# Where a hybrid attention layer finishes its mixed rows: in the merging of triangular blocks, or in the recurrence

## The reference, cut to what matters

```python
q, k, v = (silu(causal_conv4(x @ W.T)) for W in (Wq, Wk, Wv)); beta = sigmoid(x @ Wb.T)
# delta rule by chunks (q, k normalised, v and kb = k scaled by beta):
T = inverse_of_unit_triangular(kb @ k.T);  u = T @ v;  w = T @ kb
for each chunk:
    u_i = u - w @ S;  o = q @ S + masked(q @ k.T) @ u_i;  S = S + k.T @ u_i
paths  = (fir3(v), fir63(v), delta, v)
logits = gelu([x, mean and variance of each path and head] @ gate_w1.T + b1) @ gate_w2.T
probs  = floored softmax(logits / temperature, over the 4 paths)
mix    = rms_norm(sum of probs[i] * paths[i]) * onorm
x1     = layernorm(x + mix @ Wo.T)
out    = layernorm(x1 + two_of_eight_experts(x1))
```

## Time and profile before

| | |
|---|---|
| time, median of 3 runs | 1892.97 us (1891.18 to 1901.68) |
| time of the profiled execution | 1894.72 us |
| its span, first to last instruction | 1893.0 us |
| busy over the span | PE 1496.2 us (79%), DVE 1315.3 (69%), ACT 950.1 (50%), POOL 440.7 (23%) |
| granted TensorE clock, mean | 0.904 of full speed |

### The profile page before, as it was taken

How to read it: one execution, slowest core, us unless ns; L and a number is a source line. 1 busy time by engine, 2 the same in 40 slices (tenths; PEclk the granted TensorE clock), 3 DMA queues, 4 the chain that set the end, 5 groups by cost and what they waited for, 6 DMA issues and landing times. The chain is left out here.

```text
span 1893.0 us, 40332 instructions
## 1 busy us (share of the span) xinstructions
PE 1496.2 (79%) x12507; PEld 1108.8 (59%) x12508; DVE 1315.3 (69%) x3331; ACT 950.1 (50%) x1998; POOL 440.7 (23%) x473
## 2 busy tenths in 40 slices
PE   6775165979999999999999999887436999999800
PEld 3445134747747747657557567476225888888700
DVE  6995155677787887887887887875455555554488
ACT  6772061356555644654655555542443555555434
POOL 6884200000030040040030210300223333333300
PEclk9997585989999999999999999998758999999955
DMA  5558642023243243333333333232524533333295
GB/s 197 190 163 256 154 101 58 3 67 94 71 127 92 62 122 102 78 91 101 87 89 106 95 106 90 79 97 76 196 91 140 192 105 101 104 104 101 77 385 190
DMA packets 297370, 224.34 MB, mean 119 GB/s; under 512 B 173472, under 2 KB 265632, under 8 KB 296960
## 3 DMA queue, kind: packets, MB, share of 16 engines
q1 hardware_dynamic: 225600, 158.84, 29.0%
q0 software_dynamic: 15232, 43.53, 6.4%
q10 hardware_dynamic: 56384, 19.93, 4.1%
HBM read 130.42 MB, written 91.82 MB: 117 GB/s over the span
## 5 line engine op out<-in xcount | busy, mean ns | idle before, releaser
L1462 DVE SCALAR_TENSOR_TENSOR B_conv<-B_ps_x,B_cw,B_conv 128x511 f32<-128x511 f32 (+2 forms) x192 | 143.5, 748 | 65.9 <-ACT B_conv L1176 59.3
L2031 POOL DMA_INDIRECT y_d<-C_yb,C_dest x136 | 132.1, 971 | 232.0 <-ACT C_yb L2142 229.7
L422 POOL DMA_INDIRECT xs_d<-x,slot_u x128 | 133.4, 1042 | 137.4 <-DVE m_acc L1857 100.6
L688 POOL MEMSET B_z<- 128x256 f32 (+4 forms) x40 | 5.5, 191 | 674.6 <-DMA B_z<-scr_a 674.6
L1176 ACT ACTIVATE B_conv<-B_ps_x,B_cw 128x512 f32<-128x512 f32 x64 | 43.7, 683 | 167.6 <-PE B_ps_x L745 167.3
L2261 DVE TENSOR_TENSOR C_av<-C_sg,C_ps_g 128x256 f32<-128x256 f32 x136 | 57.3, 421 | 94.6 <-ACT C_sg L2136 94.6
L2065 PE MATMUL C_ps_g<-C_w_high,C_xt_high 128*128 x272 | 119.5, 439 | 0.4 <-issue 0.4
L745 PE MATMUL B_ps_x<-B_xa,B_wk 128*128 128x512 f32 x128 | 67.5, 655 | 63.8 <-DVE B_sel L1454 44.9
L2273 DVE TENSOR_TENSOR C_avt_low<-C_ps_a,C_avt_high 128x256 fp32r<-128x256 f32 x136 | 57.7, 425 | 83.5 <-ACT C_avt_high L2131 83.5
L2065 PE MATMUL C_ps_g<-C_w_high,C_xt_low 128*128 x272 | 107.7, 396 | 0.0
L2065 PE MATMUL C_ps_g<-C_w_low,C_xt_high 128*128 x272 | 107.0, 393 | 0.0
(11 more groups left out here) (330 smaller groups left out, 4250.6 us busy)
## 6 DMA issues: line engine op xcount, KB each, us to landing
C_xb<-xs_d SPq DMA_DIRECT2D x136, 132.0 KB, 2.1
C_w_high<-y_d SPq DMA_DIRECT2D x12, 1024.0 KB, 14.1
A_band<-fir_long POOLq DMA_DIRECT2D x32, 256.0 KB, 5.9
A_work<-xT SPq DMA_DIRECT2D x16, 512.0 KB, 5.0
v_d<-A_v_tok SPq DMA_DIRECT2D x16, 512.0 KB, 3.5
short_d<-A_sh_tok SPq DMA_DIRECT2D x16, 512.0 KB, 3.2
B_xa<-xT SPq DMA_DIRECT2D x8, 1024.0 KB, 5.8
B_v_tok<-v_d SPq DMA_DIRECT2D x8, 1024.0 KB, 5.5
```

What stands on the lines that cost most here:

```text
L422: pool.indirect_dma_start(t["xs_d"][:, :], bass.IndirectOffsetOnAxis(ap=slot_u[:, c:c + 1], axis=0), x1[:, b, j, :], None).then_inc(done, 16)
L1462: V.scalar_tensor_tensor(conv[:, g % 2, k:], X[g % 2][:, :SEQ - k], cw[:, g // 4, gg % CH, 3 - k:4 - k], conv[:, g % 2, k:], ALU.mult, ALU ...
L2031: pool.indirect_dma_start(t["y_d"][:, :], bass.IndirectOffsetOnAxis(ap=dest[:, q:q + 1], axis=0), yb[:, u], None).then_inc(y_out[u], 16)
```

## The change

It does five things. (a) The gate's first layer gets four banks (X[0], X[1], B3, B4): the products with x for half 0 (`from_x`) move into `stage1b`, in the place of spins; the gate itself then does the products with the statistics and half 1. (b) `turn_mix` is split. `turn_first` turns the two column blocks of half 0, through TR alone, one inside `merges` and one behind it; ACT keeps them (`keep_o(i, 0, ...)`) between its merge copies. (c) `project_out` of half 0 stands in two parts around `solve_rows(i, 0)`; `turn_second` stands behind `within(i, 0)`, and `project_out` of half 1 behind `from_state` and `project` of chunk 1. (d) In `merge_and_mix` DVE and ACT finish half 0 earlier, and in the recurrence DVE's first `add_out` moves ahead of `state(0)`. (e) The projection of group 0 of the next pair moves from the front of a step to the end of the one before, with 2 spins instead of 4; POOL's `mask_at` waits for a weighing of the mix instead of a DMA. PE's loop is one step shorter, and a further step is written out.

```diff
+        hidden = (X[0], X[1], B3, B4)
@@ POOL, mask_at
-                    pool.wait_ge(mt_in[1], 32 * (p + 1))
+                    need(pool, mixd, 4 * (p - 1) + 1)
@@ PE
+                def from_x(i, b, c):
+                    pe.wait_ge(xg_in[b], 16 * (i + 1))
+                    for k in range(CH):
+                        mm(hidden[c][:], w1x[:, k, c * P:(c + 1) * P], xg[b][:, k, :], start=k == 0, stop=False)
+                def from_stats(c):
+                    mm(hidden[c][:], w1s[:, c * P:(c + 1) * P], st_t[:], start=False, stop=True).then_inc(gate_mm, 1)
@@ PE, stage1b, behind project(p, 7) and turn_routes
-                    for g in range(5, 8):
-                        select(p, g)
-                        if last is not None:
-                            if g == 5:
-                                pe.wait_ge(a_kept[1], 4 * (p + 1))
-                            spin(B3, 2)
+                        select(p, 5)
+                        for k in a_kept:
+                            pe.wait_ge(k, 4 * (p + 1))
+                        from_x(p - 1, 0, 2)
+                        select(p, 6)
+                        from_x(p - 1, 0, 3)
+                        pe.wait_ge(taps, 24 * p + 21)
+                        from_x(p - 1, 0, 0)
+                        pe.wait_ge(taps, 24 * (p + 1))
+                        from_x(p - 1, 0, 1)
+                        select(p, 7)
+                        spin(B5, 2)
                     turn_norms(p, 1)
                     if last is not None:
                         rank(last)
-                        spin(B3, 3)
@@ PE, merges, behind the products of L919
+                    if has_prev:
+                        turn_first(i - 1, 0)
                     if has_next:
                         project(i + 1, 1)
@@ PE, recur
                     within(i, 0)
                     if has_prev:
-                        project_out(i - 1, 0)
-                        project_out(i - 1, 1)
+                        turn_second(i - 1)
                     for s in range(1, TPB):
                         from_state(i, s)
                         if has_next:
                             project(i + 1, s + 1)
...
+                        if has_prev and s == 1:
+                            project_out(i - 1, 1)
                         solve_rows(i, s)
@@ PE, gate(i, has_prev, has_next), new
+                    turn_stats(i, 0)
+                    pe.wait_ge(st_kept, 2 * i + 1)
+                    for c in range(HID_CH):
+                        from_stats(c)
+                    turn_stats(i, 1)
+                    for c in range(2):
+                        pe.wait_ge(gelu_ok, 8 * i + c + 1)
+                        from_x(i, 1, c)
...
+                    logits(i, 0)
+                    pe.wait_ge(st_kept, 2 * i + 2)
+                    for c in range(2):
+                        from_stats(c)
+                    for c in range(2, HID_CH):
+                        from_x(i, 1, c)
+                        from_stats(c)
+                    pe.wait_ge(raw_kept, 2 * i + 1)
+                    logits(i, 1)
@@ PE
+                def turn_first(i, m):
+                    pe.wait_ge(mix[0], 7 * (i + 1))
+                    if m:
+                        pe.wait_ge(o_kept, 4 * i + m)
+                    for j in range(TPB):
+                        w = nc.tensor.transpose(TR[:, j * P:(j + 1) * P], lo[:, 0, j, m * P:(m + 1) * P], ident[:])
+                    w.then_inc(o_turned, 1)
+                def turn_second(i):
+                    pe.wait_ge(mix[1], 7 * (i + 1))
+                    for m in range(CH):
+                        pe.wait_ge(ln, LN * i + m + 1)
...
+                def project_out(i, b, parts=(0, 1)):
+                    pe.wait_ge(o_kept, 4 * i + 2 * (b + 1))
+                    for jp in parts:
@@ PE, step
-                    if has_next:
-                        hold(pe, x_out, 16 * (i + 1))
-                        project(i + 1, 0)
                     merges(i, has_prev, has_next)
+                    if has_prev:
+                        turn_first(i - 1, 1)
+                        project_out(i - 1, 0, (0,))
                     pe.wait_ge(m_dve, 9 * (i + 1))
                     solve_rows(i, 0)
                     pe.wait_ge(m_act, 9 * (i + 1))
                     if has_prev:
-                        turn_mix(i - 1)
+                        project_out(i - 1, 0, (1,))
                     recur(i, has_prev, has_next)
...
                         at_rest(i + 1)
-                        spin(X[1], 4)
+                    if has_after:
+                        project(i + 2, 0)
+                        spin(X[1], 2)
@@ ACT, recur
                     keep_u(i, 0)
                     if has_prev:
-                        keep_o(i - 1)
+                        keep_o(i - 1, 1)
@@ ACT, merge_and_mix
                     weigh_values(i, 1)
                     if has_next:
-                        for k in (1, 2):
+                        merge(i + 1, 1)
+                    rms(i, 0)
+                    if has_next:
+                        for k in (2, 3):
                             merge(i + 1, k)
-                    rms(i, 0)
-                    if has_next:
-                        merge(i + 1, 3)
+                    keep_o(i, 0, (0,))
                     rms(i, 1)
                     if has_next:
                         merge(i + 1, 4)
+                    keep_o(i, 0, (1,))
@@ DVE, recur
-                    for q in range(TPB):
-                        bn(q, 2)
+                    bn(0, 2)
+                    bn(1, 2)
+                    if has_prev:
+                        add_out(i - 1, 0)
+                    bn(2, 2)
+                    bn(3, 2)
                     state(0)
                     if has_next:
                         taps_of(i + 1, 1)
                     output(0)
                     if has_prev:
-                        add_out(i - 1, 0)
                         row_stats(i - 1, 0)
@@ DVE, merge_and_mix
                     weigh(i, 1)
+                    sum_squares(i, 0)
                     if has_next:
                         merge(i + 1, 2)
+                    scale_mix(i, 0)
                     add_two(i, 1)
-                    sum_squares(i, 0)
                     if has_next:
                         merge(i + 1, 3)
-                    scale_mix(i, 0)
                     add_rest(i, 1)
```

More of the change, by code:

```diff
@@ L809, in at_products, with stage1b @@
                                 i.then_inc(at_mm, 1)
-                def stage1b(p, last=None):
+                def from_x(i, b, c):
[4 more added lines that the diff above has]
+                    mm(hidden[c][:], w1s[:, c * P:(c + 1) * P], st_t[:], start=False, stop=True).then_inc(gate_mm, 1)
+                def stage1b(p, last=None, first=False):
                     if last is not None:
@@ L844, in stage1b @@
                         turn_routes(last)
-                    for g in range(5, 8):
-                        select(p, g)
-                        if last is not None:
-                            if g == 5:
-                                pe.wait_ge(a_kept[1], 4 * (p + 1))
-                            spin(B3, 2)
+                    if first:
+                        for g in range(5, 8):
+                            select(p, g)
+                    else:
+                        select(p, 5)
[10 more added lines that the diff above has]
+                        spin(B5, 2)
                     turn_norms(p, 1)
@@ L996, in recur, with turn_stats @@
                         within(i, s)
[L998 to L1002, removed]
+                def turn_stats(i, b):
                     for j in range(TPB):
@@ L1006, in gate, with logits @@
                     w.then_inc(st_turned, 1)
-                    pe.wait_ge(xg_in[b], 16 * (i + 1))
+                def logits(i, b):
+                    pe.wait_ge(gelu_ok, 8 * i + 4 * (b + 1))
                     for c in range(HID_CH):
[L1009 to L1022, removed]
+                        w = mm(B2[c * LANE:(c + 1) * LANE, :], w2[:, c, :], hid[:, c, :], start=True, stop=True)
+                    w.then_inc(raw_mm, 1)
+                def gate(i, has_prev, has_next):
+                    if has_prev:
+                        pe.wait_ge(rt, RT * (i - 1) + 1)
+                    pe.wait_ge(st_dve, ST * (i + 1))
+                    turn_stats(i, 0)
+                    if not has_next:
+                        pe.wait_ge(taps, 24 * (i + 1))
+                        for c in range(HID_CH):
+                            from_x(i, 0, c)
+                    pe.wait_ge(st_kept, 2 * i + 1)
+                    for c in range(HID_CH):
+                        from_stats(c)
[4 more added lines that the diff above has]
+                    if has_next:
                         for k in a_kept:
@@ L1133, in step @@
                         rank(i - 1)
-                    for b in range(2):
```

(28 more changed lines are left out.)

67 lines of the change are left out of this document (29 added, 38 removed).

## The result

The changed kernel takes 1965.3 us (median; 1959.8 to 1970.1), the kernel before 1893.1 in the same comparison: ratio 1.037, 95% interval 1.033 to 1.041. It is 72 us slower; 67 were forecast. Its profiled execution spans 1968.3 us, 75.3 more than before.

A forecast was written before the change was run, and what follows sets the result against it. The ring was taken as one chain, with DVE the bound at stage1b's end and PE setting the merging's pace. 7 x 3.2 + 7 x 4.8 + 6 x 3.0 - 6.0 = +68 us on 1894.7; forecast 1960, range 1900 to 1985.

The forecast's parts named there:

- A: End of stage1b: four `from_x` groups make the last selection late, passing through norm to the next solver; +3.2 us a step.
- B: Gate and merging, up to `solve_rows(0)`: earlier start, lost clock and added work sum to +4.8 us a step.
- The earlier start: Merging: PE, freed early, starts when the triangles land at 971.0 instead of at 973.51; saves 2.3 us.
- The half clock: Merging after PE idles almost 7 us: first product +1.8, betas' products +0.9, spins behind them +1.2 us.
- the tail: Behind L928, `turn_first(1)`, ACT's copy and half of half 0's `project_out` now precede `solve_rows(0)`; +2.3 us.
- C: Chunk 0 of the recurrence: PE waits for DVE's `output(0)`, then runs partly at half clock; +3.0 us, six times.
- The seam: Between L928 and `solve_rows(0)`: clock holds by the skill page; by earlier rows it may fall, +14 us, 1974.
- Half 0 too late: Rival, merging: `scale_mix(0)` comes behind L919, so `turn_first(0)` holds L928; +10 us on top, 1970; chance 0.06.
- The prize: Rival, chunk 0: `output(0)` does not hold L951, -3.6 us a step; 1894 with clock kept, or 1872; chance 0.11.
- the earlier `mask_at` ... under the convolution: nothing: Merging: POOL's earlier mask runs in the same stretch, under the convolution, and was to cost nothing.

The follow-up runs named there:

- the loads on one queue: SP issues ACT's five triangle loads behind its own two; alone on the changed kernel: 1948.7 us, ratio 1.027 to the kernel before.
- twelve spins: Changed kernel with twelve spins instead of two ahead of the merging: 1941.1 us, ratio 1.022 to the kernel before.
- the copies later: Changed kernel with ACT's convolution of the next pair ahead of the copies of half 1's turned rows: 1916.3 us, ratio 1.009 to the kernel before.
- ten spins: The kernel with all three edits, but ten spins instead of twelve ahead of the merging: 1883.9 us, ratio 0.992 to the kernel before.
- all three edits: Changed kernel with last selection ahead of two input groups, twelve spins before merging, and ACT's convolution before half 1's copies: 1876.5 us, ratio 0.988 to before.

## Why the prediction was right

The forecast (1960) and its range hold the result, and the likeliest case was the one that happened. By its steps:

*A, +3.2.* The stretch to the next solver grew from 53.8 to 57.0, and putting the selection first gave all of it back.

*B, +4.8.* In the ring shown it is 41.71 - 36.70 = +5.0 (copy's start to `solve_rows(0)`); in the mean of six +4.6. The sum held, its split did not: the misses cancelled, which is luck. The earlier start brought 0.3 us (9.97 instead of 10.26) where 2.3 were counted; in the mean of six 1.15, most of it from the ring of pair 1 (13.27 to 8.49). I had taken the store and the loads of the ring shown before, where the second load was there 7.8 us behind the copy's start; now it was 9.55. Most of this, 1.35 us, lies with the store ahead of the loads:

```profile
scr_xt<-B_zt SPq DMA_DIRECT2D x1, 512.0 KB, 2.7
scr_xt<-B_zt SPq DMA_DIRECT2D x1, 512.0 KB, 4.1
```

The first row is of before, the second of after, with the time to landing at the end. The store had been as slow (3.8 and 3.9 us) in two other rings of before. A further 0.4 lies with the load (3.9 instead of 3.5 us), and from its landing to L899 it was 0.4, where 0.1 was counted. ACT, freed earlier, now issues its loads at 1024.65, ahead of SP's at 1025.88, where it had been behind. But over the six rings the second load took 4.0 us in both kernels, so this order is not shown to have cost anything; the loads on one queue gain because ACT's are out of the way altogether (2.8 to 3.0 us). The half clock cost 1.4 + 0.9 + 0.5 = 2.8 us (product, betas, spins) where 3.9 were counted; the ring shown is the cheapest of the six, and in their mean it cost 3.5 (from the product to `solve_rows(0)` 32.5 us, with twelve spins 29.0). In the ring shown the rest, `turn_first(0)` and the tail, is 5.0 + 0.3 - 2.8 = 2.5, where 3.2 were counted. The Trainium skill ("TensorE: Matmul & The Clock Gate", HAM oscillation — how this bites in real kernels) describes this pattern: a wait for a DMA between groups of products, after which each group starts cold. The trace agrees: a wait of 9.24 us, and products at 0.50.

*C, +3.0.* In the mean of six 23.2 - 20.5 = +2.7. `output(0)` ended 14.4 us behind `solve_rows(0)` (15.6 counted), and half clock cost 0.9 + 1.4 = 2.3 (1.8 counted).

*The seam.* The clock held, and `solve_rows(0)` took 1.90 us, so the 14 us that the earlier trace rows would have added did not come; by the Trainium skill's sentence, quoted in the prediction, none were due. The earlier trace rows were no accident either: with the turns and the projection taken away, a wait of 1.58 us brought their half clock back in two of six rings and in step 7.

*Rivals.* "Half 0 too late" did not occur: L1081 followed L937 without a wait. "The prize" turned on `output(0)` ending within about 10 us, and the experiment with the copies later met that point: chunk 0 15.9 us, against 17.2 worked out.

*What was missed.* The sum was 68, the two spans differ by 75.3 (the profiled execution is the slowest of the four; the medians differ by 72). In rings 1 to 6 I counted 66 and it was 63.2. From the last solver on I counted 4.8 - 6.0 = -1.2 and it was -3.3. In the ring of pair 0 I counted 3.2 for A alone, and it grew by 14.2 (117.5 to 131.7). The step that failed is "the earlier `mask_at` ... under the convolution: nothing": in the middle rings it lies there, in the first it meets the solver, 3.7 us. The other 7 us lie for the most part with the half clock of that ring, which I had counted in the other rings alone. Some 5 of them are the luck of this execution (126.3 us with the copies later). Part of the rest goes with (e): in the kernel before, the projection at the front of the step ran between solver and merging, and the merging began at full clock; now PE stands idle there. First before, then after:

```profile
308.71 3.69 PE L745 MATMUL B_ps_x<-B_xa,B_wk 128*128 128x512 f32 x4 [18.87 <-DMA scr_x<-B_z]
313.49 2.21 PE L881 MATMUL B_ps_b<-area 32*32 32x32 f32 x128 [1.08 <-DMA area<-scr_xt]
319.29 3.62 PE L899 MATMUL B_ps_b<-area 32*32 32x32 f32 x128 [26.42 <-DMA area<-scr_xt]
```

## What to carry to other kernels

Moving work out of a stretch pays only if what then ends last there is known: here it was a convolution, queued on ACT behind copies that were not ready, and swapping the two was worth 49 us. PE, freed early, stood idle and lost its clock: cover such a wait with work, or with spins. See which loads other engines issue beside those that the chain waits for: taking them out of the way gave 1 us a ring. Before moving work off a start, ask whether the engine that sets the pace has less to do afterwards; if not, the start moves and the end stays.

## What the runs showed of the hardware

A vector product stood still while POOL worked. In the changed kernel's first ring, where its like takes 0.39 us:

```profile
292.25 4.08 DVE L1577 TENSOR_TENSOR B_z<-B_z,B_zt 128x220 f32<-128x220 f32 x1
292.24 3.85 POOL L699 TENSOR_SCALAR_AFFINE_SELECT area<-area 128x4096 f32<-128x4096 f32 x1 [8.44 <-ACT area L1286]
```

The product ended 0.24 us behind the mask. In all eleven kernels with the early mask this product took 3.9 to 4.1 us; with the mask moved away none of that solver took over 0.41. The kernel before had the same collision elsewhere: in six of its eight steps the mask met an addition of the mix (L1725, two operands in SBUF, 1.23 us alone), which then took 2.0 to 4.1. In step 7:

```profile
1240.37 3.83 POOL L698 TENSOR_SCALAR_AFFINE_SELECT area<-area 128x4096 f32<-128x4096 f32 x1 [12.66 <-DMA area<-scr_xt]
1241.20 4.07 DVE L1725 TENSOR_TENSOR B_lo<-B_lo,B_delta 128x1024 f32<-128x1024 f32 x1
```

In a middle ring of the changed kernel the mask ran beside DVE's taps, which read one operand from PSUM, and these took their usual 0.75 us. The Trainium skill ("GPSIMD Engine Reference", Specifications) names contention with DVE instructions that have two SBUF inputs; the trace agrees, with 3.7 us for one instruction.

The slow store has a companion in the traces. With ten spins it took 4.4 us in the ring at 962 and 2.7 in the ring at 1095. In the window of the first (962.2 to 967.8) one packet of 16 KB of the queue that the profile calls "instruction" was under way; in that of the second (1095.4 to 1099.3) that queue has no row (queue: packets, MB, share of the 16 engines; a DMA's KB and time to landing):

```profile
q8 instruction: 1, 0.02, 1.1%
scr_xt<-B_zt SPq DMA_DIRECT2D x1, 512.0 KB, 4.4
scr_xt<-B_zt SPq DMA_DIRECT2D x1, 512.0 KB, 2.7
```

The profiled executions of all thirteen kernels have 104 of these stores. Of the 36 that took over 3 us, 35 had such a packet beside them or the store just ahead; of the 68 faster ones, 2. With all three edits it came ahead of both stores or 3.6 us and more behind the copy's start, when the store's packets were over (3.4), and the store took 2.7 to 2.8 us in every ring. No run moved the packet alone, so that it is the cause is not shown.
